# Four graph layers, two batches in flight: the last layer's second values, queries and keys through the other accumulators, and a new order

## The chip, the cores and the metric

The kernel runs on one core of a Trainium2 chip. The number is the device time of one launch in microseconds (us), the median of several runs. The core has a matrix engine (TensorE, PE in the rows; its weight loads are PEld), VectorE (DVE), ScalarE (ACT), GpSimd (POOL), and SyncE (SP), which issues transfers. Each engine works through its own instructions strictly in order and meets the others only at semaphores.

## The reference, cut to what matters

16 batches of 512 nodes with 256 features pass through four layers, each followed by a residual sum and a layer norm.

```python
x = _layernorm(x + _L0_gnn_ref(x, adj, w, a1, a2))      # attention from two scores per node, elu
x = _layernorm(x + _L1_gnn_ref(x, adj, ...))             # 3 times: attention, norm, 256-1024-256 gelu ffn, norm
x = _layernorm(x + _L2_gnn_ref(x, adj, W, a))            # like L0, keeping the 16 largest weights of a row
x = _layernorm(x + _L3_gnn_ref(x, adj, Wq, Wk, Wv, Wo))  # 8 heads of 32 features
...
q = heads(x @ Wq); k = heads(x @ Wk); v = heads(x @ Wv)
scores = jnp.einsum('bhnd,bhmd->bhnm', q, k) / sqrt_dk
attn = jax.nn.softmax(jnp.where(mask, scores, -jnp.inf), axis=-1)
out = jnp.einsum('bhnm,bhmd->bhnd', attn, v)
return jax.nn.relu(out) @ Wo
```

## The kernel before

**Tiles.** A batch is four row tiles of 128 nodes; tiles 0 and 1 are half 0, tiles 2 and 3 half 1. All of a batch's work is cut into named *stages*, such as `v1` (the values of half 1) or `pT0` (transposing the weights of tile 0). Each engine has a table from stage names to the code that it runs for them; a stage in which an engine has no part is skipped there.

**Two batches in flight.** Two slots, A and B, each hold one batch with buffers of its own (in printed rows, the first number of `work_1_0` or `acc_1_0` is the slot, and the one in `XT_1` too; the profile leaves these numbers out). The list `HALF` is one half turn: the batch in one slot does its *middle* (layer L0, then L1.0, then L1.1 and the first attention of L1.2), while the batch in the other slot does its *ending* (the ffn of L1.2, L2, L3) and the next one is *starting*. The order of the entries of `HALF` is the order of the instructions on every engine, so moving one entry moves it on all that take part. A turn runs `to_a`, then `to_b`, seven times in a loop, with an opening half turn (middle alone, mostly) ahead, and a closing one behind, which is followed by an ending that runs alone. That makes 16 half turns with a middle in them, of which 15 also have an ending.

**Banks.** TensorE writes to eight banks: for each slot, two *work* banks, used in strict alternation in the order of the list `uses` (class `Use`), and two *accumulators* (`acc`), used in the order of `acc_uses`. Before TensorE writes to a bank it waits until the engine that read the last contents has freed it (`evacuated`), and readers wait for `filled`. In L3 the head scores of a *quad* (four heads by one row tile) need all four banks of the slot at once: `sq{q}` on TensorE writes them, `sq{q}` and `sr{q}` on VectorE add the mask and take the row minimum (line 867), `ex{n}` on ScalarE is the exponential (line 1036), `uT{n}` transposes a head's weights (line 1270), and `pv{g}` multiplies them by the values (line 1289).

**Around the change.** `qk0` and `qk1` compute the queries and keys of feature chunk 0 and 1 (four heads each, line 1238). ScalarE copies the queries out (line 1025), VectorE the keys (`keys`, line 854). `v0` and `v1` compute the values (line 1130, copied by ScalarE, line 956). Before, all of them go through the two work banks, and in that list `v1`, `q`, `k` of chunk 1 stand behind `scores 0`, the first quad. The middle's stages next to them are those of L1.1: `sx1` (node scores on VectorE, line 671), `bc` (their broadcast by TensorE, line 1161), `zs0`/`zs1` (sums on ScalarE, line 964), `mx0`/`mx1` (mask, row minimum, leaky relu on VectorE, lines 692 to 704), `exp0`/`exp1` (line 978), `pT0` to `pT3` (transposes, line 1173, copied by lines 752 and 986), `agg0`/`agg1` (weights times rows, line 1187). The ffn's stages are `hT` (transpose, line 1103), `f1hq` (first product, half h, quarter q, line 1209, gelu on line 1018), and `f2hq` (second product, line 1223). `sum`, `norm`, `xsum`, `xnorm` are sums with statistics, and normalizations, on VectorE, with a power on GpSimd between them (line 510); `xa1` is an affine step on GpSimd (lines 518, 522), in L1.0 with an addition to all of `X1` behind it (line 560). `masks` and `load` belong to the transfers.

## Time and profile before

| what | value |
| --- | --- |
| time, median of 3 runs | 3801.18 us (3792.32 to 3809.88) |
| the profiled execution | 3815.43 us, of which 3813.8 us from the first to the last instruction |
| mean granted TensorE clock | 0.961 of full speed |
| TensorE busy | 3324.7 us, 87% |
| VectorE busy | 2460.1 us, 65% |
| ScalarE busy | 2204.2 us, 58% |
| GpSimd busy | 773.0 us, 20% |
| table loads on ScalarE | 198 |

TensorE is busy for most of the span, so its idle times, and the stretches at the lower clock, are what an order can change. The others' shares are averages over stages in which sometimes one and sometimes another of them is what TensorE waits for. A "half turn" in the rows is the stretch from one `v1` of L0 to the next.

### The profile page before, as it was taken

What the parts mean: (1) busy time and instruction counts of PE and PEld (TensorE: products, weight loads), DVE (VectorE), ACT (ScalarE), POOL (GpSimd) and SP (SyncE); (2) the same over time, 40 slices, a digit from 0 to 9 for tenths busy, and PEclk for the clock granted to TensorE, in tenths of its full rate; (3) what the DMA queues carried; (4) which work ended last, traced back from release to release, by engine and by line L of the source; (5) the groups of instructions that cost most, each with busy time, mean ns of one, the idle gap of its engine ahead of it and who ended that gap; (6) DMA issues with size and microseconds to landing.
All of it is one profiled execution on the core that took longest, in us unless ns stands there. A gap on an engine that the chain in (4) does not pass through costs nothing.

```text
span 3813.8 us, 59841 instructions
## 1 busy us (share of the span) xinstructions
PE 3324.7 (87%) x18048; PEld 2558.3 (67%) x18048; DVE 2460.1 (65%) x7151; ACT 2204.2 (58%) x4349; POOL 773.0 (20%) x1052
## 2 busy tenths in 40 slices
PE   6689989898898899889998898989989898899866
PEld 4576766767667676666766677676766766667653
DVE  3466676666757666676666767666676666767654
ACT  3256556665565756656665575756656665565623
POOL 1212122121211222121121212122121121211210
PEclk8899999999999999999999999999999999999988
DMA  5000000000000000000000000000000000000000
GB/s 137 1 1 12 7 12 7 7 7 7 12 7 10 3 7 12 7 12 7 7 7 7 12 7 12 1 7 12 7 12 7 7 6 7 12 7 1 1 6 6
DMA packets 39858, 40.24 MB, mean 11 GB/s; under 512 B 7264, under 2 KB 38240, under 8 KB 39520
## 3 DMA queue, kind: packets, MB, share of 16 engines
q1 hardware_dynamic: 31072, 27.68, 2.4%
q0 software_dynamic: 8448, 8.39, 1.5%
q8 instruction: 170, 2.79, 0.3%
q14 instruction: 168, 1.38, 0.1%
HBM read 36.07 MB, written 8.39 MB: 12 GB/s over the span
## 4 chain that ended last, share of the span: by engine, by line
PE 48%; issue 25%; ACT 11%; DVE 11%; POOL 4%; DVEq 0%; DMA 0%; POOLq 0%; ACTq 0%; SPq 0%
PE acc L1187 11%; PE work L1209 9%; PE acc L1223 7%; PE acc L1289 3%; PE work L1130 3%; ACT PT L1036 3%; PE acc L1258 3%; POOL rstd L510 2%; PE acc L1270 2%; PE acc L1318 2%; PE work L1103 2%; PE work L1238 2%; ACT L1036 2%; PE work L1173 1%; DVE stats L759 1%
## 5 line engine op out<-in xcount | busy, mean ns | idle before, releaser
L1209 PE MATMUL work<-XT,w_sb 128*128 128x256 f32 x3072 | 732.7, 384 | 36.7 <-DVE XT L816 15.0
L510 POOL TENSOR_TENSOR rstd<-var_eps,minus_half 128x2 f32<-128x2 f32 x320 | 225.1, 703 | 2641.4 <-DVE var_eps L768 2641.2
L1223 PE MATMUL acc<-w_sb,gT 128*128 128x256 f32 x3072 | 731.4, 385 | 0.0
L1209 PEld LDWEIGHTS work<-XT,w_sb 128*128 128x128 f32 x3072 | 557.6, 190 | 168.2 <-ACT gT L1018 35.5
L1223 PEld LDWEIGHTS acc<-w_sb,gT 128*128 128x128 f32 x3072 | 579.9, 193 | 97.8 <-issue 22.8
L1018 ACT ACTIVATE gT<-work,b_sb 128x256 f32<-128x256 f32 x768 | 343.1, 473 | 208.6 <-PE work L1209 201.1
L1187 PE MATMUL acc<-X,PT 128*128 128x256 f32 x1536 | 387.6, 410 | 24.8 <-ACT PT L986 24.2
L1187 PEld LDWEIGHTS acc<-X,PT 128*128 128x128 f32 x1536 | 312.7, 207 | 108.8 <-issue 46.3
L1018 ACT ACT_TABLE_LOAD x198 | 254.0, 1283 | 3.5
L752 DVE COPY PT<-work 128x512 f32<-128x512 f32 x160 | 109.5, 684 | 225.5 <-PE work L1173 223.8
L759 DVE BATCH_NORM_STATS2 stats<-R 128x6 f32<-128x256 f32 x640 | 240.9, 418 | 11.0
L1173 PE MATMUL work<-ident,T 128*128 128x128 f32 x1280 | 184.1, 282 | 72.9 <-ACT T L978 56.6
L1187 PE MATMUL acc<-V,PT 128*128 128x256 f32 x1024 | 235.8, 383 | 3.9 <-ACT PT L986 3.7
L1173 PEld LDWEIGHTS work<-ident,T 128*128 128x128 f32 x1280 | 146.8, 143 | 123.2 <-ACT T L978 91.2
L699 DVE SCALAR_TENSOR_TENSOR T<-T 128x512 f32<-128x512 f32 x320 | 225.3, 708 | 0.0
L1258 PE MATMUL acc<-X,R 32*128 32x512 f32 x512 | 154.7, 678 | 75.9 <-DVE X L854 44.4
L692 DVE CUSTOM_DVE_ANT_0 T<-T,pos 128x512 f32<-128x512 f32 x256 | 186.9, 766 | 50.5 <-ACT T L964 50.2
L1187 PEld LDWEIGHTS acc<-V,PT 128*128 128x128 f32 x1024 | 196.1, 192 | 33.3 <-issue 4.5
L978 ACT ACTIVATE T<-T,neg_max 128x512 f32<-128x512 f32 x256 | 182.4, 713 | 59.4 <-DVE neg_max L704 59.0
L1047 ACT ACTIVATE PT<-acc 128x512 f32<-128x512 f32 x128 | 76.1, 594 | 241.7 <-PE acc L1270 241.7
L956 ACT ACTIVATE V<-work 128x258 f32<-128x258 f32 (+1 forms) x192 | 74.1, 386 | 234.5 <-PE work L1130 234.5
L986 ACT ACTIVATE PT<-work 128x512 f32<-128x512 f32 x160 | 93.9, 587 | 172.1 <-PE work L1173 170.9
(153 smaller groups left out, 5934.7 us busy)
## 6 DMA issues: line engine op xcount, KB each, us to landing
HX<-in_x SPq DMA_DIRECT2D x16, 512.0 KB, 3.8
pos<-in_adj POOLq DMA_DIRECT2D x16, 512.0 KB, 5.7
out<-X SPq DMA_DIRECT2D x32, 256.0 KB, 2.1
w_sb<-in_L_gnn_W SPq DMA_DIRECT2D x6, 1024.0 KB, 8.4
g_sb<-in_L_gnn_g SPq DMA_DIRECT2D x6, 128.0 KB, 6.7
awr_sb<-in_L_gnn_attn_w SPq DMA_DIRECT2D x2, 256.0 KB, 7.9
c_sb<-in_L_gnn_beta SPq DMA_DIRECT2D x3, 128.0 KB, 4.5
PT<-in_L_gnn_b SPq DMA_DIRECT2D x3, 128.0 KB, 5.7
```

The source lines that it names most:

```text
L510: pool.tensor_tensor(rstd[s][:, half_rows(half)], var_eps[s][:, half_rows(half)], minus_half[:], ALU.pow)\
L692: dve.tensor_tensor_reduce(T[s][:, t, :], T[s][:, t, :], pos[s][:, t, :], 1.0, HIGHEST, ALU.add, ALU.min, neg_row[s][:, t:t + 1]).then_inc ...
L699: dve.scalar_tensor_tensor(T[s][:, t, :], T[s][:, t, :], ALPHA[key], T[s][:, t, :], ALU.mult, ALU.max if key == "L2" else ALU.min).then_in ...
L759: last = dve.bn_stats(stats[s][:, t, :], R[s][:, t, :])
L978: act.activation(to, T[s][:, t, :], ACT.Exp, bias=neg_max[s][:, t:t + 1], scale=1.0 if key == "L2" else -1.0, accum_out=den[s][:, t:t + 1] ...
L1018: act.activation(gT[s][:, f, :], u.bank[:, 0:HN], ACT.Gelu, bias=b1_sb[:, l, f:f + 1]).then_inc(u.evacuated, 1)
L1036: act.activation(z, z, ACT.Exp, bias=head_min[s][:, n:n + 1], scale=-1.0, accum_out=den3[s][:, m, half * HT + i, r:r + 1]).then_inc(exp_do ...
L1173: last = pe.transpose(u.bank[:, j * P:(j + 1) * P], T[s][:, t, j * P:(j + 1) * P], ident[:])
L1187: last = pe.matmul(acc[s][half][:, t % HT, :], PT[s][:, j, t * P:(t + 1) * P], src[s][:, j, 0:D], start=(j == 0 and t % HT == 0), stop=(j ...
L1209: last = pe.matmul(u.bank[:, 0:HN], w1_sb[:, l, c, f * P:(f + 1) * P], XT[s][:, c, half * HN:(half + 1) * HN], start=(c == 0), stop=(c == ...
L1223: last = pe.matmul(acc[s][half][:, i, :], gT[s][:, f, i * P:(i + 1) * P], w2_sb[:, l, f, :], start=(f == 0 and i == 0), stop=(f == FC - 1) ...
L1258: pe.matmul(use.bank, q_sb[s][rows, m, t * P:(t + 1) * P], k_sb[s][rows, m, :], start=True, stop=True).then_inc(use.filled, 1)
```

## The change

Three things.

1. `v1` of L3 no longer uses the work banks: its two tiles go to the slot's two accumulators. So do the queries and the keys of chunk 1. In `uses`, these four entries are gone, and the two `q`/`k` entries that stay are those of chunk 0; in `acc_uses`, `v1 L3` and `qk1 L3` stand ahead of `scores 0`.
2. Since the banks are used in list order, `v1` and `qk1` now come ahead of the first quad `sq0` in `HALF`.
3. The rest of `HALF` is in a new order too, in about twenty places. The stages and the work in them are the same.

```diff
-        ("middle", "L1.0", "xnorm1"), ("ending", "L3", "qk0"), ("middle", "L1.1", "sx1"),
-        ("ending", "L3", "sq0 sr0"), ("middle", "L1.0", "xa1"), ("middle", "L1.1", "bc zs0 mx0"),
-        ("ending", "L3", "v1"), ("middle", "L1.1", "zs1 exp0 mx1"), ("ending", "L3", "qk1"),
...
+        ("middle", "L1.1", "sx1"), ("ending", "L3", "load qk0 v1 qk1 sq0 sr0"), ("middle", "L1.0", "xa1"),
+        ("middle", "L1.1", "bc zs0 mx0 zs1 exp0"), ("ending", "L3", "ex0"), ("middle", "L1.1", "mx1"),
...
-        uses += [("xT0 L3", DC), ("v0 L3", HT), ("xT1 L3", DC), ("q L3", 1), ("k L3", 1), ("scores 0", 2), ("v1 L3", HT), ("q L3", 1), ("k L3", 1)]
+        uses += [("xT0 L3", DC), ("v0 L3", HT), ("xT1 L3", DC), ("q0 L3", 1), ("k0 L3", 1), ("scores 0", 2)]
...
-        acc_uses = [(k, 1) for k in ["L0"] + [k + c for k in L1K for c in ("", " ffn")] + ["L2"]] + [("scores 0", 1)]
+        acc_uses = [(k, 1) for k in ["L0"] + [k + c for k in L1K for c in ("", " ffn")] + ["L2"]]
+
+        acc_uses += [("v1 L3", 1), ("qk1 L3", 1), ("scores 0", 1)]
...
+        def query_or_key(s, it, m, i):
+
+            return HeadUse(s, it, 2 + i, ("q0 L3", "k0 L3")[i], 0) if m == 0 else HeadUse(s, it, i, "qk1 L3")
...
             def keys(m):
                 def stage(s, it, key):
-                    u = Use(s, it, "k L3", m)
-                    dve.wait_ge(u.filled, u.turn)
-                    dve.tensor_copy(k_sb[s][:, m, :], u.bank[:]).then_inc(u.evacuated, 1)
+                    use = query_or_key(s, it, m, 1)
+                    dve.wait_ge(use.filled, use.filled_at)
+                    dve.tensor_copy(k_sb[s][:, m, :], use.bank).then_inc(use.evacuated, 1)
...
                     for t in tiles(half):
-                        u = Use(s, it, "v L0", t) if key == "L0" else Use(s, it, f"v{half} {key}", t % HT)
-                        pe.wait_ge(u.evacuated, u.turn)
+                        if key == "L3" and half == 1:
+                            use = HeadUse(s, it, t % HT, "v1 L3")
+                            pe.wait_ge(use.evacuated, use.free)
+                            bank, made = use.bank, use.filled
```

**First place, TensorE, the start of L3 in slot 1.** Before, behind the first queries and keys come the first quad (line 1258, to all four banks), the broadcast of L1.1 in slot 0 (line 1161), and only then the values (line 1130), which need a work bank of the quad back.

```order
L1238 MATMUL work_1_0<-XT_1,wq_sb 128x512 x2
L1238 MATMUL work_1_1<-XT_1,wk_sb 128x512 x2
...
L1258 MATMUL work_1_0<-X_1,R_1 128x512
L1258 MATMUL work_1_1<-X_1,R_1 128x512
L1152 REGISTER_ALU
L1161 MATMUL work_0_1<-ident,s12_0 128x128 x4
L1128 REGISTER_ALU
L1130 MATMUL work_1_0<-wv_sb,XT_1 128x256 x2
L1130 MATMUL work_1_1<-wv_sb,XT_1 128x256 x2
L1236 REGISTER_ALU
L1238 MATMUL work_1_0<-XT_1,wq_sb 128x512 x2
L1238 MATMUL work_1_1<-XT_1,wk_sb 128x512 x2
```

The same engine and place with the change (the same lines have other numbers in the changed file: values 1145, queries and keys 1253, quad 1273, broadcast 1176, transposes of L1.1 1188).

```order
L1253 MATMUL work_1_1<-XT_1,wk_sb 128x512 x2
...
L1145 MATMUL acc_1_0<-wv_sb,XT_1 128x256 x2
...
L1253 MATMUL acc_1_0<-XT_1,wq_sb 128x512 x2
L1251 REGISTER_ALU
L1253 MATMUL acc_1_1<-XT_1,wk_sb 128x512 x2
...
L1273 MATMUL work_1_1<-X_1,R_1 128x512
L1167 REGISTER_ALU
L1176 MATMUL work_0_1<-ident,s12_0 128x128 x4
L1184 REGISTER_ALU
L1188 MATMUL work_0_0<-ident,T_0 128x128 x4
```

The values and the second queries and keys, which stood between the broadcast and the transposes of L1.1, stand ahead of the quad now, and nothing is left between the broadcast and the transposes that wait for its results.

**Second place, ScalarE, L0 of slot 0 beside the ffn of L1.2 in slot 1.** Before, the sums of tiles 0 and 1 (line 964, `zs0`) stand ahead of the gelus of `f102` (line 1018), and those of tiles 2 and 3 (`zs1`) behind them.

```order
L1008 ACTIVATE XT_1<-work_1_1,beta1t_sb,g1t_sb 128x256
L962 REGISTER_ALU
L964 ACTIVATE T_0<-work_0_0,V_0 128x512 x2
L1017 REGISTER_ALU
L1018 ACTIVATE gT_1<-work_1_1,b1_sb 128x256
L1017 REGISTER_ALU
L1018 ACTIVATE gT_1<-work_1_0,b1_sb 128x256
L964 ACTIVATE T_0<-work_0_0,V_0 128x512 x2
L968 ISA
L1018 ACTIVATE gT_1<-work_1_1,b1_sb 128x256
```

With the change (sums 973, gelu 1027):

```order
L1017 ACTIVATE XT_1<-work_1_1,beta1t_sb,g1t_sb 128x256
L971 REGISTER_ALU
L973 ACTIVATE T_0<-work_0_0,V_0 128x512 x4
L977 ISA
L1026 REGISTER_ALU
L1027 ACTIVATE gT_1<-work_1_1,b1_sb 128x256
L1026 REGISTER_ALU
L1027 ACTIVATE gT_1<-work_1_0,b1_sb 128x256
L1027 ACTIVATE gT_1<-work_1_1,b1_sb 128x256
```

All four sums now run ahead of the first gelu of `f102`. On TensorE, their broadcast `bc` of L0 has moved from behind `hT1` to between `hT0` and `f100`.

**Third place, TensorE, L1.0 of slot 0 beside L2 of slot 1.** Before, the values of L2 (line 1130) stand ahead of `agg1` of L1.0 (line 1187).

```order
L1103 MATMUL work_1_0<-ident,X1_1 128x128 x2
L1119 REGISTER_ALU
L1130 MATMUL work_1_1<-wg_sb,XT_1 128x258 x2
L1130 MATMUL work_1_0<-wg_sb,XT_1 128x258 x2
L1179 REGISTER_ALU
L1187 MATMUL acc_0_1<-X1_0,PT_0 128x256 x4
L1185 REGISTER_ALU
L1187 MATMUL acc_0_1<-X1_0,PT_0 128x256 x4
```

With the change (transposes 1112, values 1145, `agg1` 1202):

```order
L1112 MATMUL work_1_0<-ident,X1_1 128x128 x2
L1194 REGISTER_ALU
L1202 MATMUL acc_0_1<-X1_0,PT_0 128x256 x4
L1200 REGISTER_ALU
L1202 MATMUL acc_0_1<-X1_0,PT_0 128x256 x4
L1209 REGISTER_ALU
L1112 MATMUL work_0_1<-ident,HX_0 128x128 x2
L1112 MATMUL work_0_0<-ident,HX_0 128x128 x2
L1128 REGISTER_ALU
L1145 MATMUL work_1_1<-wg_sb,XT_1 128x258 x2
L1145 MATMUL work_1_0<-wg_sb,XT_1 128x258 x2
```

The values moved behind `agg1` and `hT0` of L1.0. On VectorE, at the same time, `sum0` of L1.0 goes ahead of L2's copy of `XT`, and `mx0` of L2 goes behind `norm1` and `hT1` of L1.0. A little later `f203` goes ahead of `agg0` of L2.

## Rows read from the trace of the kernel before

**Rows 1.** The page's first part: busy time, share, instructions of TensorE.
```profile
PE 3324.7 (87%) x18048; PEld 2558.3 (67%) x18048; DVE 2460.1 (65%) x7151; ACT 2204.2 (58%) x4349; POOL 773.0 (20%) x1052
```
**Rows 2.** Windows of two half turns: stretch, its length, busy times, granted clock.
```profile
887.70:1118.20 230.50, 206.70 (x1130) 158.85 (x1128) 154.15 (x448) 139.69 (x274) 48.86 (x66) 0.97 0.03 8
1806.40:2034.20 227.80, 203.60 (x1129) 157.47 (x1128) 154.16 (x449) 139.69 (x274) 49.11 (x67) 0.99 0.03 8
```
**Rows 3.** Timeline of TensorE, start of L3: start, length, what [idle before, releaser].
```profile
1000.39 1.95 PE L1238 MATMUL work<-XT,wq_sb 128*128 128x512 f32 x4 [0.56 <-DVE XT L654]
...
1005.23 0.70 PE L1258 MATMUL acc<-X,R 32*128 32x512 f32 x2 [1.17 <-DVE X L854]
...
1006.42 0.65 PE L1161 MATMUL work<-ident,s 128*128 128x128 f32 x4
1008.49 1.99 PE L1130 MATMUL work<-wv_sb,XT 128*128 128x256 f32 x8 [1.42 <-DVE head_min L867]
1010.32 1.88 PE L1238 MATMUL work<-XT,wq_sb 128*128 128x512 f32 x4
...
1013.83 0.66 PE L1173 MATMUL work<-ident,T 128*128 128x128 f32 x4
1015.03 0.66 PE L1173 MATMUL work<-ident,T 128*128 128x128 f32 x4 [0.55 <-ACT T L978]
1017.38 1.22 PE L1258 MATMUL acc<-X,R 32*128 32x512 f32 x2 [1.70 <-DVE X L854]
...
1019.40 5.88 PE L1187 MATMUL acc<-X,PT 128*128 128x256 f32 x16
```
**Rows 4.** Timeline of VectorE at the same place.
```profile
1006.51 0.69 DVE L867 CUSTOM_DVE_ANT_0 T<-acc,pos 128x512 f32<-128x512 f32 x1
...
1008.96 1.04 DVE L692 CUSTOM_DVE_ANT_0 T<-T,pos 128x512 f32<-128x512 f32 x1
...
1013.99 0.68 DVE L692 CUSTOM_DVE_ANT_0 T<-T,pos 128x512 f32<-128x512 f32 x1
...
1016.56 0.68 DVE L854 COPY X<-work 128x512 f32<-128x512 f32 x1
```
**Rows 5.** Timeline of ScalarE at the same place.
```profile
1014.16 0.72 ACT L978 ACTIVATE T<-T,neg_max 128x512 f32<-128x512 f32 x1 [0.39 <-DVE neg_max L704]
...
1016.06 0.72 ACT L978 ACTIVATE T<-T,neg_max 128x512 f32<-128x512 f32 x1 [0.60 <-DVE neg_max L704]
...
1017.48 0.57 ACT L986 ACTIVATE PT<-work 128x512 f32<-128x512 f32 x1
```
**Rows 6.** A window at the same place: length, busy times, granted clock.
```profile
1017.00:1023.80 6.80, 6.42 (x18) 4.08 (x19) 3.48 (x11) 3.88 (x11) 0.00 (x0) 0.50 0.00 1
```
**Rows 7.** Timeline of TensorE, L0 beside the ffn of L1.2.
```profile
890.91 3.72 PE L1209 MATMUL work<-XT,w_sb 128*128 128x256 f32 x16 [0.64 <-DVE XT L816]
...
895.91 3.88 PE L1209 MATMUL work<-XT,w_sb 128*128 128x256 f32 x16
...
902.61 1.43 PE L1173 MATMUL work<-ident,T 128*128 128x128 f32 x8 [1.10 <-ACT T L978]
```
**Rows 8.** Timeline of ScalarE at the same place.
```profile
895.11 0.56 ACT L1008 ACTIVATE XT<-work,beta1t_sb,g1t_sb 128x256 f32<-128x256 f32 x1
896.11 1.27 ACT L964 ACTIVATE T<-work,V 128x512 f32<-128x512 f32 x2 [0.43 <-PE work L1161]
...
900.45 1.28 ACT L978 ACT_TABLE_LOAD   x1
```
**Rows 9.** Timeline of TensorE, L1.0 beside L2.
```profile
959.15 1.99 PE L1209 MATMUL work<-XT,w_sb 128*128 128x256 f32 x8 [0.95 <-ACT gT L1018]
962.00 0.66 PE L1103 MATMUL work<-ident,HX 128*128 128x128 f32 x4 [0.86 <-DVE HX L773]
```
**Rows 10.** Timeline of ScalarE, L2's first aggregation read out.
```profile
984.77 0.60 ACT L986 ACTIVATE PT<-work 128x512 f32<-128x512 f32 x1
```
**Rows 11.** Timeline of TensorE, the ending that runs alone.
```profile
3733.11 2.91 PE L1130 MATMUL work<-wv_sb,XT 128*128 128x256 f32 x8 [2.21 <-DVE head_min L867]
```

More of the change, by code:

```diff
@@ L349, in build, with __init__ @@
         class HeadUse:
-            def __init__(self, s, it, place, name):
+            def __init__(self, s, it, place, name, n=None):
                 if place < 2:
@@ L358, in __init__ @@
                 else:
[L359 removed]
+                    u = Use(s, it, name, place - 2 if n is None else n)
                     self.bank, self.filled, self.filled_at = u.bank[:], u.filled, u.turn
                     self.evacuated, self.free, self.done = u.evacuated, u.turn, u.turn + 1
+        def query_or_key(s, it, m, i):
+            return HeadUse(s, it, 2 + i, ("q0 L3", "k0 L3")[i], 0) if m == 0 else HeadUse(s, it, i, "qk1 L3")
         def target_score(s, key, t):
@@ L952, in stage @@
                     for t in tiles(half):
+                        if key == "L3" and half == 1:
+                            use = HeadUse(s, it, t % HT, "v1 L3")
+                            act.wait_ge(use.filled, use.filled_at)
+                            act.activation(V[s][:, t, 0:D], use.bank[:, 0:D], ACT.Copy).then_inc(use.evacuated, 1)
+                            continue
                         u = Use(s, it, "v L0", t) if key == "L0" else Use(s, it, f"v{half} {key}", t % HT)
@@ L1022, in stage @@
                 def stage(s, it, key):
-                    u = Use(s, it, "q L3", m)
-                    act.wait_ge(u.filled, u.turn)
-                    act.activation(q_sb[s][:, m, :], u.bank[:], ACT.Copy, scale=-float(DK) ** -0.5).then_inc(u.evacuated, 1)
+                    use = query_or_key(s, it, m, 0)
+                    act.wait_ge(use.filled, use.filled_at)
+                    act.activation(q_sb[s][:, m, :], use.bank, ACT.Copy, scale=-float(DK) ** -0.5).then_inc(use.evacuated, 1)
                 return stage
@@ L1126, in stage @@
                     for t in tiles(half):
-                        u = Use(s, it, "v L0", t) if key == "L0" else Use(s, it, f"v{half} {key}", t % HT)
-                        pe.wait_ge(u.evacuated, u.turn)
+                        if key == "L3" and half == 1:
+                            use = HeadUse(s, it, t % HT, "v1 L3")
+                            pe.wait_ge(use.evacuated, use.free)
+                            bank, made = use.bank, use.filled
+                        else:
+                            u = Use(s, it, "v L0", t) if key == "L0" else Use(s, it, f"v{half} {key}", t % HT)
+                            pe.wait_ge(u.evacuated, u.turn)
+                            bank, made = u.bank, u.filled
                         for c in range(DC):
-                            last = pe.matmul(u.bank[:, 0:columns], XT[s][:, c, t * P:(t + 1) * P], weights[:, c, 0:columns],
+                            last = pe.matmul(bank[:, 0:columns], XT[s][:, c, t * P:(t + 1) * P], weights[:, c, 0:columns],
                                              start=(c == 0), stop=(c == DC - 1))
-                        last.then_inc(u.filled, 1)
+                        last.then_inc(made, 1)
                 return stage
@@ L1233, in stage @@
                         wait_transposed(s, it, key, 1)
-                    for name, w in (("q", wq_sb), ("k", wk_sb)):
-                        u = Use(s, it, f"{name} L3", m)
-                        pe.wait_ge(u.evacuated, u.turn)
+                    for i, w in enumerate((wq_sb, wk_sb)):
+                        use = query_or_key(s, it, m, i)
+                        pe.wait_ge(use.evacuated, use.free)
                         for c in range(DC):
-                            last = pe.matmul(u.bank[:], w[:, c, m * P:(m + 1) * P], XT[s][:, c, :],
+                            last = pe.matmul(use.bank, w[:, c, m * P:(m + 1) * P], XT[s][:, c, :],
                                              start=(c == 0), stop=(c == DC - 1))
-                        last.then_inc(u.filled, 1)
+                        last.then_inc(use.filled, 1)
                 return stage
@@ L1247, in stage @@
                     if q % (NQ // DC) == 0:
-                        for name in "qk":
-                            use = Use(s, it, f"{name} L3", m)
-                            pe.wait_ge(use.evacuated, use.turn + 1)
+                        for part in range(2):
+                            use = query_or_key(s, it, m, part)
+                            pe.wait_ge(use.evacuated, use.done)
                     places = [HeadUse(s, it, r, f"scores {q}") for r in range(HPC)]
```

1 line of the change is left out of this document (removed), and 101 rows, old and new, of the table HALF.

## The prediction

> **What bounds the kernel now.** First read the page: TensorE is busy for 3324.7 of 3813.8 us [rows 1], so it is the engine whose idle time and clock the order can change. Next cut the span into half turns. Two of them, 230.50 and 227.80 us long [rows 2], do the same work; TensorE is busy for 206.70 us in one and 203.60 in the other, at a granted clock of 0.97 and 0.99. So some 24 us of a half turn are idle, and a further 3 come and go with the clock. Then read TensorE's timeline at the places that the change touches, asking for each idle stretch what ends it, and read VectorE and ScalarE beside it: what counts is which of them is late.
>
> At the start of L3 [rows 3] the idle stretches are 1.17 us (the key copy, line 854), 1.42 (the row minima of the quad, line 867, that hold the work banks), 0.55 (an exponential of L1.1), and 1.70 (the second key copy). VectorE is what is late: from the first row minimum at 1006.51 [rows 4] to the key copy at 1016.56 it has one operation behind another. Behind the four idle stretches the granted clock is 0.50, its lower level of 1.2 GHz, for the whole window from 1017.0 to 1023.8 [rows 6], and `agg0` of L1.1 takes 5.88 us [rows 3], where its 16 products last some 3.6 at full clock, by the x16 row of 3.72 of the same shape [rows 7].
>
> **The change, part by part.** All times are of the half turn that the rows show, and "shift" is how much later a stage comes with the change.
>
> *The start of L3.* The same products are issued, in as many instructions; nothing is removed but two waits. The 1.42 us wait for the row minima goes, since the values use banks long free, and the 1.70 us wait goes, since the second keys are copied before the quad. But two things are lost. The copy of the second keys must now be over before the quad starts, which is the 1.17 us wait again, only later. And the values with the second queries and keys took from 1008.49 to 1013.83, 5.3 us [rows 3], between the broadcast and `pT0`, in which sums, mask and exponential of L1.1 ran. With the change nothing is left there. Step by step, with the shift at entry set to nought: first queries and keys from 1000.4, 3.5 us (as 1010.32 to 1013.83), to 1003.9; values 1.8 (1008.49 to 1010.32), to 1005.7; second queries and keys 3.5, to 1009.2; wait 1.2; quad 1.2 (1005.23 to 1006.42), to 1011.6; broadcast 0.6, to 1012.2. VectorE's first row minimum comes 1.3 us after the quad's start (1005.23 in [rows 3], 1006.51 in [rows 4]), so at 1011.7, and the four take 2.45 (1006.51 to 1008.96), to 1014.15. Then `mx0`, in the same order on VectorE as before: an undisturbed `mx` takes 2.57 us (1013.99 to 1016.56 in [rows 4]), and the first exponential starts 2.07 us after its beginning (1013.99 there, 1016.06 in [rows 5]). So exponential at 1016.2, and `pT0` 0.87 later (1014.16 in [rows 5], 1015.03 in [rows 3]), at 1017.1. TensorE is idle from 1012.2 to 1017.1, 4.9 us. `mx1` ends at 1014.15 + 5.15 = 1019.3; ScalarE's copy of `pT0` starts 0.92 after the end of `mx1` (1016.56 in [rows 4], 1017.48 in [rows 5]), lasts 0.57, and `agg0` starts at 1020.9. Before, it started at 1019.40 [rows 3]. So this place costs 1.5 us by itself.
>
> In this sum `mx0` runs undisturbed. Before, its first operation took 1.04 us, where the same in `mx1` takes 0.68 [rows 4]; GpSimd's additions to `X1` (line 560) ran then. They follow `sx1`, which now comes before the key copies, so they are over by about 1012. If they were not, the price would be that of `mx0` before, 5.03 us (1008.96 to 1013.99) less 2.57, so 2.5 more. The Trainium skill (SBUF — State Buffer, "SBUF: two separate sides") says that VectorE with two inputs in SBUF and GpSimd hold a shared port pair in turn, and that the other fully blocks. The trace shows a stretched operation beside GpSimd, as that rule has it, but by less than a full GpSimd operation; by the rule alone the sum would be the 2.5 higher if the two met again.
>
> *L1.0 beside L2.* The values of L2 stood in front of `agg1` of L1.0; now they stand behind `hT0`, and fill the time in which its transpose is waited for. `mx0` of L2 leaves its place ahead of `norm1` of L1.0, which `hT1` waited 0.86 us for, after 0.95 ahead of `f101` [rows 9]. `agg1` comes earlier by the values' 1.8 us and by the 0.5 us that they waited for their copy; of `f101`'s and `hT1`'s waits about 1.4 us go, and new ones of 0.5 (ahead of `hT0`) and of 0.6 (a gelu now behind the sums) come. With the values themselves paid later, `f102` comes about 2.5 us earlier. Not all stays. `f203` now stands ahead of `agg0` of L2, so `agg0` ends only 0.7 us or so earlier, and ScalarE's read of it, a table load of 1.28, and the copy of `pT2` (984.77, 0.60 long) [rows 10] follow it; `agg1` of L2 needs that copy. I get 1.0 us of new idle time there. So L3 begins with a shift of -1.5.
>
> *L0 beside the ffn of L1.2.* The broadcast now fills 0.43 us of the 0.64 us gap ahead of `f100` [rows 7]. But on ScalarE all four sums come before the first gelu of `f102`. They start when the copy of `hT1` is done, 895.67 [rows 8], and two take 1.27, four 2.4, so to 898.1. The gelu then frees its bank at 898.6; `f103`, which is the second half of the x16 row at 895.91 and began at 897.8 [rows 7], needs it. It comes 0.8 us later, its last gelu ends at 901.05, and the table load for the exponential starts then, not at 900.45 [rows 8]: +0.6 for `pT0` of L0, which already waited for it (1.10 us in [rows 7]). TensorE is busy from there on, so +0.6 stays.
>
> *The small swaps* (`uT8`, `uT18`, `pT2`, `ex14` and the like), one price together: ScalarE and VectorE have slack where these stand, so they are taken at nothing, except `uT8`, whose earlier place pushes `hT1` of L1.1 against a gelu: +0.2. Without that slack each would cost one copy, about 0.6 us [rows 10].
>
> *The ending that runs alone.* There the wait ahead of the values is 2.21 us [rows 11], with no middle to hide it; the same walk gives about -1 once.
>
> **The sum.** Per half turn +0.6 (L0) -1.5 (to the start of L3) +1.5 (start of L3) +0.2 = +0.8. Fifteen half turns have both parts: +12, and -1 for the last ending, so +11 us: 3824.8 for the profiled span of 3813.8. The profiled execution lies 14 us above the median of the runs shown, 3801.18, so the forecast is 3801.18 + 11 = **3812 us**. In this the clock's loss is left as it is. That is the largest unknown: the lower clock now costs about 5.88 - 3.6 = 2.3 us at `agg0` and 0.9 at the slowed quad ahead of it. With more of TensorE's idle time in one piece it may fall earlier, inside that piece, and cost less, or last longer. Bounds: all of the 2.3 gained, or, as much again lost.
>
> **The rivals.**
>
> *The lower clock falls into the new idle stretch (faster).* For it: the stretch of 4.9 us comes before the place where the clock fell, so `agg0` could run at full clock again. Against it: there is still idle time right ahead of `agg0`. Price: -2.3 in each of 15 half turns, -35: 3777 us. It decides for faster once more than 2.0 us per half turn come back in this way.
>
> *The lower clock lasts longer (slower).* Here the 4.9 us bring the clock down earlier and the second idle piece, between the second quad and `agg0`, keeps it down: `agg0` in full and the first transposes at half speed, +1.5 per half turn; and the few half turns that now keep their clock, like that of 227.80 us [rows 2], lose their 2.7 us too (three or so, 8 us). 15 x 1.5 + 8 = 30 on top of 11: 3842 us. The Trainium skill (TensorE: Matmul & The Clock Gate, "What's actually happening") says the gate follows how busy the array has been recently. By that rule a longer idle piece speaks for this rival; that the clock fell behind four idle stretches here agrees [rows 3, 6].
>
> *Nothing much at all (no change).* The 1.5 us lost at the start of L3 rest on VectorE starting the minima only after the late quad. If the walk misses 0.8 us per half turn, from L0's gelu and from there, the time is 3801. This is also the case that the change does what it says, removing the two waits, and the removed time turns up as one wait for `pT0`.
>
> **How the numbers follow.** I give the forecast (3800 to 3824 for its own range, half a microsecond or so per half turn either way) 0.37, no change at all 0.17, the clock falling earlier 0.22, the clock lasting longer 0.24. A measurement of this kernel tells about 0.5%, 19 us, from no change: under 3782 counts as faster, over 3820 as slower. Faster takes the first rival and a little of the rest, 0.24; slower takes the second and the upper end of the forecast, 0.33; the remaining 0.43 is same. The range for 8 in 10 runs from the first rival's price, 3775, to the second's, 3842.
>
> **What would show it.** Right: no wait of the values for line 867's successor any more; an idle stretch of 4 to 6 us ahead of `pT0` of L1.1, ended by ScalarE's exponential; the second quad without a wait; `f103` of L1.2 waiting about 1 us for a gelu; `hT1` of L1.0 about 2 us earlier in the half turn. Half turns of about 231 us. Wrong: the idle ahead of `pT0` stays under 3 us, which would mean VectorE reaches `mx0` sooner than the walk has it; or the granted clock at `agg0` of L1.1 is at its full level in most half turns.

## The result, and the profile after

The changed kernel takes **3819.67 us** (median of 12 runs, 3812.31 to 3827.39), the kernel before 3801.69 us beside it (12 runs, 3790.56 to 3809.88): a ratio of **1.0051**, 95% interval 1.0038 to 1.0065, so 18 us slower where 11 were forecast.

The profiled execution of before (3815.43 us) lies above all 12 timed runs of before, so its span and that of the changed kernel's profile (3818.62 us, near its median) are only 3 us apart. Its waits are those of other executions, but its mean clock (0.961) is under that of all 10 runs of `same_again`. Another execution of the kernel before, `same_again` (3796.67 us, span 3795.0), is the fairer partner for totals, and is used so below.

First the page of the changed kernel, which answers to [rows 1]:

```profile
span 3817.0 us, 59925 instructions
PE 3338.0 (87%) x18048; PEld 2564.3 (67%) x18048; DVE 2417.6 (63%) x7151; ACT 2198.5 (58%) x4349; POOL 747.7 (20%) x1052
```

And that of the kernel before in its other execution:

```profile
span 3795.0 us, 59841 instructions
PE 3311.0 (87%) x18048; PEld 2555.5 (67%) x18048; DVE 2459.8 (65%) x7151; ACT 2204.3 (58%) x4349; POOL 773.7 (20%) x1052
```

Subtract TensorE's busy time from the span: it idles for 479.0 us after the change and 484.0 before it. Idle time went down by 5 us. The same 18048 instructions were busy for 27 us longer. The granted clock went down with it (mean 0.952 to 0.957 in the 12 runs of the changed kernel, 0.962 to 0.966 in the 10 of `same_again`), by about 1%, and 27 us are 0.8% of the busy time. So the loss is one of clock.

TensorE's timeline of the changed kernel at the start of L3, to be laid beside [rows 3] (columns: start, length, what, idle before it and its releaser):

```profile
994.39 1.95 PE L1253 MATMUL work<-XT,wq_sb 128*128 128x512 f32 x4 [0.56 <-DVE XT L658]
...
997.90 1.89 PE L1145 MATMUL acc<-wv_sb,XT 128*128 128x256 f32 x8
999.63 1.88 PE L1253 MATMUL acc<-XT,wq_sb 128*128 128x512 f32 x4
1001.35 1.88 PE L1253 MATMUL acc<-XT,wk_sb 128*128 128x512 f32 x4
1004.01 0.70 PE L1273 MATMUL acc<-X,R 32*128 32x512 f32 x2 [0.79 <-DVE X L858]
...
1005.08 0.65 PE L1176 MATMUL work<-ident,s 128*128 128x128 f32 x4
1010.72 1.97 PE L1188 MATMUL work<-ident,T 128*128 128x128 f32 x8 [4.98 <-ACT T L987]
1012.62 1.22 PE L1273 MATMUL acc<-X,R 32*128 32x512 f32 x2
...
1014.72 4.70 PE L1202 MATMUL acc<-X,PT 128*128 128x256 f32 x16
```

The waits of 1.42, 0.55 and 1.70 us are gone, that of 1.17 is 0.79, and 4.98 us stand ahead of `pT0`. From the first queries to `agg0` it takes 20.33 us; before, 19.01 [rows 3].

VectorE there, beside [rows 4]: the minima start when the late quad is there, and `mx0` (line 696) runs undisturbed.

```profile
1003.26 0.69 DVE L858 COPY X<-acc 128x512 f32<-128x512 f32 x1 [2.85 <-PE acc L1253]
1005.32 0.69 DVE L871 CUSTOM_DVE_ANT_0 T<-acc,pos 128x512 f32<-128x512 f32 x1 [1.36 <-PE acc L1273]
1007.77 0.69 DVE L696 CUSTOM_DVE_ANT_0 T<-T,pos 128x512 f32<-128x512 f32 x1
```

The clock of the changed kernel in windows (start and end, length, busy time of PE, PEld, DVE, ACT, POOL, then the granted clock, the DMA share and GB/s), to be laid beside [rows 2] and [rows 6]:

```profile
1003.20:1009.90 6.70, 1.75 (x13) 0.72 (x12) 5.27 (x16) 2.48 (x5) 2.40 (x4) 1.00 0.00 0
1009.90:1016.70 6.80, 5.96 (x21) 3.70 (x22) 5.58 (x17) 6.18 (x17) 0.00 (x0) 0.50 0.00 1
1016.70:1023.50 6.80, 6.36 (x45) 5.08 (x43) 3.25 (x10) 3.60 (x10) 0.00 (x0) 1.00 0.00 0
881.70:1112.10 230.40, 206.86 (x1131) 159.35 (x1129) 151.38 (x449) 139.35 (x275) 47.19 (x66) 0.97 0.03 8
```

The clock is at its upper level for most of the idle stretch (which runs from 1005.73 to 1010.72) and falls to 1.2 GHz 0.8 us before its end. It stays there over `pT0`, `pT1`, the second quad and the first products of `agg0`, and is back for the rest of `agg0`. The same holds in all 14 half turns that follow the first: the clock falls inside the idle stretch, 0.1 to 2.9 us before its end.

L0 on TensorE and ScalarE, beside [rows 7, 8]:

```profile
893.06 1.99 PE L1224 MATMUL work<-XT,w_sb 128*128 128x256 f32 x8 [0.98 <-ACT gT L1027]
897.75 1.43 PE L1188 MATMUL work<-ident,T 128*128 128x128 f32 x8 [0.96 <-ACT T L987]
```

```profile
889.93 2.41 ACT L973 ACTIVATE T<-work,V 128x512 f32<-128x512 f32 x4
892.53 0.84 ACT L1027 ACTIVATE gT<-work,b_sb 128x256 f32<-128x256 f32 x2 [0.18 <-ACT T L973]
895.58 1.28 ACT L987 ACT_TABLE_LOAD   x1
```

The four sums run for 2.41 us, `f103` waits 0.98 us for the gelu behind them, and `pT0` of L0 starts 16.05 us after the half turn's start at 881.70, where it was 14.91 (902.61 in [rows 7] less 887.70 in [rows 2]): +1.14.

### The profile page after: what moved, and what is told of

It reads as the page before. It is cut to its first block, busy times and chain, and to the rows that moved or that the text cites. A ratio compares the mean times of both kernels' runs of the same rounds, so it can differ in the third digit from the quotient of the medians.

```text
span 3817.0 us, 59925 instructions
## 1 busy us (share of the span) xinstructions
PE 3338.0 (87%) x18048; PEld 2564.3 (67%) x18048; DVE 2417.6 (63%) x7151; ACT 2198.5 (58%) x4349; POOL 747.7 (20%) x1052
## 4 chain that ended last, share of the span: by engine, by line
PE 42%; issue 33%; DVE 10%; ACT 9%; POOL 5%; DVEq 0%; DMA 0%; POOLq 0%; ACTq 0%; SPq 0%
PE acc L1238 8%; PE work L1224 5%; PE acc L1202 5%; PE acc L1304 3%; PE acc L1273 3%; POOL rstd L514 3%; PE work L1145 3%; ACT PT L1045 2%; PE acc L1333 2%; PE acc L1285 2%; PE work L1188 2%; PE work L1112 2%; PE work L1253 2%; DVE stats L763 2%; ACT L1045 2%
## 5 line engine op out<-in xcount | busy, mean ns | idle before, releaser
L1202 PE MATMUL acc<-X,PT 128*128 128x256 f32 x1536 | 371.1, 397 | 25.0 <-ACT PT L995 24.8
L1202 PEld LDWEIGHTS acc<-X,PT 128*128 128x128 f32 x1536 | 298.8, 199 | 105.3 <-ACT PT L995 32.9
L1188 PE MATMUL work<-ident,T 128*128 128x128 f32 x1280 | 204.9, 296 | 143.5 <-ACT T L987 124.2
L1188 PEld LDWEIGHTS work<-ident,T 128*128 128x128 f32 x1280 | 159.9, 151 | 189.4 <-ACT T L987 144.9
L703 DVE SCALAR_TENSOR_TENSOR T<-T 128x512 f32<-128x512 f32 x320 | 217.3, 683 | 0.0
L973 ACT ACTIVATE T<-work,s 128x512 f32<-128x512 f32 x192 | 116.2, 690 | 121.8 <-PE work L1176 121.8
```

What stands on the lines that cost most here:

```text
L703: dve.scalar_tensor_tensor(T[s][:, t, :], T[s][:, t, :], ALPHA[key], T[s][:, t, :], ALU.mult, ALU.max if key == "L2" else ALU.min).then_in ...
L1188: last = pe.transpose(u.bank[:, j * P:(j + 1) * P], T[s][:, t, j * P:(j + 1) * P], ident[:])
L1202: last = pe.matmul(acc[s][half][:, t % HT, :], PT[s][:, j, t * P:(t + 1) * P], src[s][:, j, 0:D], start=(j == 0 and t % HT == 0), stop=(j ...
```

## The experiments

The theory (the "order theory" of the expectations) was the prediction's: three sites of +0.6, -1.5 and +1.5 us per half turn, limited at the start of L3 by VectorE's queue. The rivals: the clock alone (the "clock theory"); no effect of an order; the broadcast, which comes too late behind the quad, as the limit. Ratios are to the kernel before on the same chip (3793.36 us in the first set, 3800.25 in the second, 3796.69 in the third).

### First set: the parts apart

`same_again` is the kernel before, unchanged.

> The kernel before, unchanged, to see how far its own executions lie apart in the granted clock. Both theories: ratio 1.000 within 0.002. The order theory says that the places of the lower clock are the same in every execution (agg0 of L1.1 in most half turns), the clock theory that some executions lose it in fewer half turns, with a time some 10 us under the 3815 us of the profiled execution shown.

Measured 1.0012 (0.9994 to 1.0030): no difference.

`l0_back` is the changed kernel with the old order of L0:

```diff
-        ("middle", "L0", "v1"), ("ending", "L1.2", "hT0 ha0"), ("middle", "L0", "bc"),
-        ("ending", "L1.2", "sum1 norm1 f100 f101 hT1 ha1"), ("middle", "L0", "zs0 mx0 zs1"),
-        ("ending", "L1.2", "f102 f103"), ("middle", "L0", "exp0"), ("ending", "L1.2", "f200"),
+        ("middle", "L0", "v1"), ("ending", "L1.2", "hT0 ha0 sum1 norm1 f100 f101 hT1"),
+        ("middle", "L0", "bc zs0"), ("ending", "L1.2", "ha1"), ("middle", "L0", "mx0"),
+        ("ending", "L1.2", "f102"), ("middle", "L0", "zs1"), ("ending", "L1.2", "f103"),
...
```

> The changed kernel with the old order in L0 alone (the stages ahead of L2's xT0). Order theory: the comparison of the two traces puts TensorE 1.1 us later at the end of this part in every half turn, so undoing it gives back 15 to 16 times 1.1, 17 us: about 3803 us, ratio 1.000. Clock theory (the loss is the clock's alone, from the 5 us idle stretch in L3): no more than 4 us come back, 3816 us, ratio 1.004.

Measured 1.0028 (1.0013 to 1.0043), against 1.0051 for the whole change: the order of L0 costs about 0.0023, 9 us, which is the forecast's 15 times 0.6. The two intervals just overlap, so this size is a rough one. The order theory's 1.000 lies outside the interval, since the rest of the change costs more than it had. The clock theory's 1.004 lies inside it, but that theory has no place for a loss in L0 itself, which the waits show (the 0.98 us of `f103` are gone from TensorE's rows of `l0_back`).

`acc_alone` is the change with the old order everywhere except at the start of L3:

```diff
-        ("middle", "L1.0", "xnorm1"), ("ending", "L3", "qk0"), ("middle", "L1.1", "sx1"),
-        ("ending", "L3", "sq0 sr0"), ("middle", "L1.0", "xa1"), ("middle", "L1.1", "bc zs0 mx0"),
-        ("ending", "L3", "v1"), ("middle", "L1.1", "zs1 exp0 mx1"), ("ending", "L3", "qk1"),
+        ("middle", "L1.0", "xsum1 xnorm1"), ("middle", "L1.1", "sx1"),
+        ("ending", "L3", "load qk0 v1 qk1 sq0 sr0"), ("middle", "L1.0", "xa1"),
+        ("middle", "L1.1", "bc zs0 mx0 zs1 exp0"), ("ending", "L3", "ex0"), ("middle", "L1.1", "mx1"),
```

> The kernel before with the accumulators for v1 and qk1 and the changed order from xsum1 of L1.0 to the second quad of L3, and the old order everywhere else. Order theory: agg0 of L1.1 starts 1.6 us later per half turn, 15 times that is +24 us, less 1.0 to 1.5 us per half turn for an agg0 at the full clock: 3803 to 3811 us, ratio 1.000 to 1.0025. If TensorE's clock brings no relief: 3825 us, 1.006. If VectorE's removed waits counted for themselves (1.4 + 1.7 us less idle time per half turn): 3755 us, 0.988.

Measured 1.0100 (1.0067 to 1.0133): 38 us, over all three expectations. TensorE's timeline shows the same walk as in the whole change, with `agg0` at full clock here:

```profile
1017.43 1.97 PE L1190 MATMUL work<-ident,T 128*128 128x128 f32 x8 [4.98 <-ACT T L989]
1019.33 1.22 PE L1275 MATMUL acc<-X,R 32*128 32x512 f32 x2
...
1021.44 3.72 PE L1204 MATMUL acc<-X,PT 128*128 128x256 f32 x16
```

Again 20.33 us from the queries (at 1001.11) to `agg0`. Against `same_again`, TensorE idles 15.5 us more (499.5 of 3835.1) and is busy 24.6 us more (3335.6). The idle part is the walk's, somewhat less than the 22 us forecast; the busy part is the clock. What the walk stands against is seen in TensorE's rows of `same_again`:

```profile
995.78 1.96 PE L1238 MATMUL work<-XT,wq_sb 128*128 128x512 f32 x4 [0.56 <-DVE XT L654]
...
1012.77 0.70 PE L1258 MATMUL acc<-X,R 32*128 32x512 f32 x2 [1.70 <-DVE X L854]
...
1013.84 3.72 PE L1187 MATMUL acc<-X,PT 128*128 128x256 f32 x16
```

There it is 18.06 us, with the second quad 0.70 and `agg0` 3.72, not 1.22 and 5.88 as in [rows 3]. The waits of the stretch add up to 5.77 us after the change (0.79 and 4.98) and 4.83 in `same_again` (1.17, 1.41, 0.55 and 1.70). So of the 2.27 us between 18.06 and 20.33 some 0.9 are idle time and the rest, about 1.3, is that of the halved clock on the transposes and the second quad. Read over the 14 half turns that follow the first, `agg0` of L1.1 lasts over 5 us in 11 of them in the profile of before, in 6 in `same_again`, and in none in the changed kernel; the stretch to it is 20.3 us long in 13 of the changed kernel's and 18.1 or 18.2 in 9 of those of `same_again`. And `proj0` with `pv3`, late in the half turn, last 6.2 us on average in the changed kernel, 5.5 in `same_again`.

`l1_order_alone` is the kernel before with the new order from `xT0` of L2 to `xT1` of L3 alone:

```diff
-        ("middle", "L1.0", "agg0 pT2 pT3"), ("ending", "L2", "xT1 v1"),
-        ("middle", "L1.0", "sum0 norm0 agg1 hT0 ha0 sum1"), ("ending", "L2", "bc zs0 mx0"),
-        ("middle", "L1.0", "norm1 f100 f101 hT1"), ("ending", "L2", "zs1"),
+        ("middle", "L1.0", "pT2 pT3 sum0"), ("ending", "L2", "xT1"),
+        ("middle", "L1.0", "norm0 agg1 hT0 ha0"), ("ending", "L2", "v1"),
+        ("middle", "L1.0", "sum1 norm1 f100"), ("ending", "L2", "bc zs0"),
+        ("middle", "L1.0", "f101 hT1 ha1"), ("ending", "L2", "mx0 zs1"),
...
```

> The kernel before with the changed order of L1.0 and L2 alone (xT0 of L2 to xT1 of L3). Order theory: 2.0 us per half turn gained there, as the two traces stand, and kept: 3801.7 - 31 = 3771 us, ratio 0.992. Rival: L3's start is bound by VectorE, which takes the gain back as idle time of TensorE ahead of the quad: 3800 us, ratio 1.000.

Measured **0.9931** (0.9908 to 0.9954): 26 us faster, as the order theory had it, and its rival's 1.000 falls. This part of the change is good by itself. The three parts also add up: -0.0069, +0.0100 and +0.0023 make +0.0054, and the whole change measured +0.0051.

### Second set: what limits the start of L3

All four stand on `l0_back` (1.0028). `bc_only` puts the broadcast and its first sums ahead of the second queries and keys; `bc_mask_early` puts `mx0` ahead of them too; `agg_first` and `agg_first_b` bring the transposes and `agg0` of L1.1 ahead of the quad's follow-up. The lines are those of `l0_back` in `HALF`; below them stand the stages of the same stretch in each run, in short form.

```diff
-        ("ending", "L3", "load qk0 v1 qk1 sq0 sr0"), ("middle", "L1.0", "xa1"),
-        ("middle", "L1.1", "bc zs0 mx0 zs1 exp0"), ("ending", "L3", "ex0"), ("middle", "L1.1", "mx1"),
...
```

```text
bc_only:       load qk0 v1 | xa1 | bc zs0 | qk1 sq0 sr0 | mx0 zs1 exp0 | ex0 | mx1 | ex1 | exp1 pT0 pT1
bc_mask_early: load qk0 v1 | xa1 | bc zs0 mx0 | qk1 sq0 sr0 | zs1 exp0 | ex0 | mx1 | ex1 | exp1 pT0 pT1
agg_first:     load qk0 v1 | xa1 | bc zs0 mx0 | qk1 | zs1 exp0 pT0 mx1 pT1 | sq0 sr0 | exp1 agg0 | ex0 ex1
agg_first_b:   load qk0 v1 | xa1 | bc zs0 mx0 | qk1 | zs1 exp0 pT0 pT1 | sq0 sr0 ex0 | mx1 | ex1 | exp1 agg0
```

> The kernel with L0's old order, and in L3's start the broadcast of L1.1 and the sums of zs0 moved ahead of the second queries and keys; VectorE's order is as in the change. If VectorE's late start (second key copy, then quad, minima, mask) sets when agg0 begins, the empty stretch on TensorE only moves, and the ratio stays at 1.003, as without this move. If what costs is that nothing hides the chain broadcast, sums, mask, exponential, this start of it 4 us earlier brings 3 us or so per half turn: ratio 0.991.

Measured 1.0044 (1.0025 to 1.0063). The broadcast came 5 us earlier and `pT0` no sooner, 17.0 us behind the first queries (at 997.61) where it was 16.3:

```profile
1003.06 0.65 PE L1180 MATMUL work<-ident,s 128*128 128x128 f32 x4
...
1007.93 0.70 PE L1277 MATMUL acc<-X,R 32*128 32x512 f32 x2 [0.79 <-DVE X L862]
...
1014.64 1.97 PE L1192 MATMUL work<-ident,T 128*128 128x128 f32 x8 [5.56 <-ACT T L991]
```

It is VectorE, which takes the quad's minima (from 1009.24) and only then `mx0` (from 1011.69), that `pT0` waits for. The theory of the broadcast fell.

> As bc_only, and the mask and leaky relu of tiles 0 and 1 (mx0) ahead of the second key copy on VectorE, where the change leaves VectorE idle for some 2.9 us. If VectorE's total work between sx1 and agg0 is the limit: mx0 fills the idle time, but runs beside GpSimd's additions and is stretched, the key copy and quad come later, net 0 to 1 us per half turn: ratio 0.999 to 1.003. If the empty stretch ahead of pT0 itself is the cost, 4 to 5 us per half turn go: 0.985.

Measured 1.0068 (1.0046 to 1.0090): a miss, above both expectations. TensorE's rows (first queries at 999.86):

```profile
1012.29 0.70 PE L1277 MATMUL acc<-X,R 32*128 32x512 f32 x2 [2.89 <-DVE X L862]
...
1013.36 1.64 PE L1192 MATMUL work<-ident,T 128*128 128x128 f32 x8
...
1020.17 5.59 PE L1206 MATMUL acc<-X,PT 128*128 128x256 f32 x16 [1.81 <-ACT PT L999]
```

`pT0` comes 2.8 us earlier than in `l0_back` and the first quad 2.8 us later, and `agg0` starts 20.3 us behind the queries, as it did without the move. That is what a limit in VectorE's total work predicts. But `agg0` now lasts 5.4 us or more in all 14 half turns, where it was 3.7 to 4.5 in `l0_back`. TensorE idles 8.5 us more (480.8 against 472.3) and is busy 18.4 more (3346.9 against 3328.5): the larger part of this loss is the clock's.

> The quad's minima are taken out of agg0's way: sq0 and its minima come behind the masks and transposes of L1.1 (VectorE: mx0, key copy, mx1, copy of pT1, then minima), and the second quad behind agg0, so that the product of 3.6 us runs while VectorE works through the minima. Order theory (VectorE's queue ahead of agg0 is the cost): agg0 starts some 5 us earlier, part of it given back before agg1, 3 to 5 us per half turn: ratio 0.983 to 0.991. Rival: the heads' chain becomes late instead and takes it all back: 1.003.

Measured 1.0059 (1.0035 to 1.0083); the rival's side, and above it. TensorE's idle time fell to 458.0 us from the 472.3 of `l0_back`, and `agg0` starts 14.4 us behind the queries in most half turns and not 20.3, so the order did what it was meant to do. But TensorE's busy time rose from 3328.5 to 3372.5, at a mean clock of 0.947 in the profiled execution against 0.955: the loss is mostly one of clock. VectorE's and GpSimd's rows show why the idle time fell by no more:

```profile
1009.58 1.21 DVE L699 CUSTOM_DVE_ANT_0 T<-T,pos 128x512 f32<-128x512 f32 x1
...
1011.84 0.67 DVE L711 SCALAR_TENSOR_TENSOR neg_max<-neg_row 128x1 f32<-128x1 f32 x1
```

```profile
1011.34 4.18 POOL L567 TENSOR_TENSOR X<-X,beta_sb 128x256 f32<-128x256 f32 x4
```

`mx0` has met GpSimd's affine step (1009.03 to 1011.37) and its additions to `X1` again; 0.69 became 1.21. And behind it the heads' chain is late:

```profile
1027.96 1.33 PE L1288 MATMUL work<-ident,T 128*128 128x128 f32 x8 [1.36 <-DVE head_min L874]
1030.16 1.16 PE L1276 MATMUL acc<-X,R 32*128 32x512 f32 x2 [0.88 <-DVE PT L885]
...
1033.05 1.97 PE L1288 MATMUL acc<-ident,PT 128*128 128x128 f32 x8 [0.84 <-DVE head_min L874]
```

> As agg_first, but the minima of the first quad ahead of mx1, so that agg0 waits for both on VectorE and the heads' exponentials start earlier. Order theory: agg0 comes 2.4 us later than in agg_first, while the heads are earlier: 1 to 3 us per half turn better than L0's old order alone, ratio 0.990 to 0.998. Rival as there: 1.003.

Measured 1.0146 (1.0118 to 1.0174), the worst of all; a miss. `agg0` starts as early as in `agg_first` (14.4 us behind the queries), but in the half turn read above the second quad comes 2.4 us later (21.4 against 19.0), with an idle stretch of 1.91 us ahead of `pT2`. Against `l0_back` TensorE idles only 3.8 us more (476.0) and is busy 56.5 more (3385.0): nearly all of this loss too is in the busy time, at a mean clock of 0.946. So in the last three of these four runs the larger part of the loss against `l0_back` is in TensorE's busy time, and not in its waits.

### Third set: the values alone, and GpSimd's additions out of the way

`v1_alone` has only `v1` in the accumulators, in the order of before but with `v1` behind `qk0`:

```diff
-        ("middle", "L1.0", "xnorm1"), ("ending", "L3", "qk0"), ("middle", "L1.1", "sx1"),
-        ("ending", "L3", "sq0 sr0"), ("middle", "L1.0", "xa1"), ("middle", "L1.1", "bc zs0 mx0"),
-        ("ending", "L3", "v1"), ("middle", "L1.1", "zs1 exp0 mx1"), ("ending", "L3", "qk1"),
...
+        ("ending", "L3", "qk0 v1"), ("middle", "L1.1", "sx1"), ("ending", "L3", "sq0 sr0"),
+        ("middle", "L1.0", "xa1"), ("middle", "L1.1", "bc zs0 mx0 zs1 exp0 mx1"), ("ending", "L3", "qk1"),
...
-        uses += [("xT0 L3", DC), ("v0 L3", HT), ("xT1 L3", DC), ("q L3", 1), ("k L3", 1), ("scores 0", 2), ("v1 L3", HT), ("q L3", 1), ("k L3", 1)]
+        uses += [("xT0 L3", DC), ("v0 L3", HT), ("xT1 L3", DC), ("q0 L3", 1), ("k0 L3", 1), ("scores 0", 2), ("q1 L3", 1), ("k1 L3", 1)]
...
+        acc_uses += [("v1 L3", 1), ("scores 0", 1)]
```

> The kernel before with only v1 of L3 through the accumulators and ahead of the first quad; the second queries and keys stay in the work banks and behind the quad, and the order is the old one elsewhere. If VectorE's queue from the first quad's minima to agg0 is what bounds this stretch: the values (1.8 us) fill TensorE's 1.17 us gap ahead of the quad, but the quad starts 0.6 us later and so does all behind it, up to +9 us, ratio 1.000 to 1.0025. If TensorE's idle time counts for itself: 1.2 us less per half turn, 3783 us, ratio 0.995.

Measured 1.0051 (1.0028 to 1.0074): the sign of the VectorE theory, twice its size.

```profile
1001.90 1.98 PE L1256 MATMUL work<-XT,wq_sb 128*128 128x512 f32 x4 [1.56 <-DVE head_min L874]
...
1006.89 1.36 PE L1191 MATMUL work<-ident,T 128*128 128x128 f32 x8 [1.28 <-ACT T L990]
1009.91 1.22 PE L1276 MATMUL acc<-X,R 32*128 32x512 f32 x2 [1.66 <-DVE X L861]
...
1011.93 5.83 PE L1205 MATMUL acc<-X,PT 128*128 128x256 f32 x16
```

The wait for the minima is merely handed to the queries (1.56 us), and TensorE's idle time is that of `same_again` within a microsecond (484.9 and 484.0). Its busy time is 17.7 us more (3328.7), and `agg0` lasts 4.9 us or more in 13 of 14 half turns; the mean clock of its 7 runs is 0.958 to 0.963, under most of those of `same_again`. So between these two executions the loss is the clock's, and not the later start that the VectorE theory had: its sign was right for another reason.

`shift_late` is `l1_order_alone` with GpSimd's four additions to `X1` moved from behind `xa1` to behind `mx1`, where VectorE has done with its masks:

```diff
-                    if key == L1K[0] and half == 1:
-                        for t in range(NT):
-                            last = pool.tensor_tensor(X1[s][:, t, :], X1[s][:, t, :], beta2_sb[:, L - 1, :], ALU.add)
-                        last.then_inc(x1_shifted.sems[s], 1)
...
+            def shift_x1(s, it, key):
+                if key == L1K[1]:
+                    pool.wait_ge(lrelu_done.sems[s], lrelu_done.value(it, key, NT - 1))
+                    for t in range(NT):
+                        last = pool.tensor_tensor(X1[s][:, t, :], X1[s][:, t, :], beta2_sb[:, L - 1, :], ALU.add)
+                    last.then_inc(x1_shifted.sems[s], 1)
...
+            stages = {"load": load_next, "mx1": shift_x1, ...
```

> The kernel before with the changed order of L1.0 and L2 (as l1_order_alone, 0.993), and GpSimd's four additions to X1 after VectorE's masks of L1.1 and not beside them. If the stretched mask operations (5.0 us for mx0, where mx1 takes 2.6) are on the path: agg0 of L1.1 starts 1.5 to 2.5 us earlier, ratio 0.983 to 0.987. If TensorE would not be free for it, or the additions only stretch what comes behind: 0.993.

Measured **0.9818** (0.9791 to 0.9844), 3727.8 us: 69 us faster than the kernel before, and by the ratios 2.3% under the changed kernel, a little better than expected. Against `l1_order_alone` TensorE idles 23.7 us less (429.5 of 3723.0 against 453.2 of 3763.0) and is busy 16.3 less (3293.5 against 3309.8). What it removed stands in VectorE's and GpSimd's rows of `l1_order_alone`:

```profile
994.83 1.20 DVE L695 CUSTOM_DVE_ANT_0 T<-T,pos 128x512 f32<-128x512 f32 x1
...
997.09 0.68 DVE L707 SCALAR_TENSOR_TENSOR neg_max<-neg_row 128x1 f32<-128x1 f32 x1
```

```profile
994.30 4.65 POOL L563 TENSOR_TENSOR X<-X,beta_sb 128x256 f32<-128x256 f32 x4
```

and what it left, in those of `shift_late`:

```profile
986.22 0.68 DVE L698 CUSTOM_DVE_ANT_0 T<-T,pos 128x512 f32<-128x512 f32 x1
...
987.44 0.14 DVE L710 SCALAR_TENSOR_TENSOR neg_max<-neg_row 128x1 f32<-128x1 f32 x1
```

```profile
990.84 2.78 POOL L567 TENSOR_TENSOR X<-X,beta_sb 128x256 f32<-128x256 f32 x4 [5.10 <-DVE T L705]
```

VectorE is 34 us less busy in all (2415.1 against 2449.2), and TensorE's timeline of `shift_late` shows what that frees:

```profile
976.69 1.95 PE L1244 MATMUL work<-XT,wq_sb 128*128 128x512 f32 x4 [0.56 <-DVE XT L660]
...
984.79 1.99 PE L1136 MATMUL work<-wv_sb,XT 128*128 128x256 f32 x8 [1.42 <-DVE head_min L873]
...
990.05 1.04 PE L1179 MATMUL work<-ident,T 128*128 128x128 f32 x8
991.58 0.70 PE L1264 MATMUL acc<-X,R 32*128 32x512 f32 x2 [0.49 <-DVE X L860]
```

The wait of 1.42 us that the change set out to remove is still there; the 0.55 is gone and the 1.70 is 0.49. `agg0` starts 16.0 us after the queries and lasts 3.7 us in all 14 half turns; the lower clock does not appear in this stretch in any of them.

`shift_late_bc0` adds the early broadcast of L0 (behind `ha0` of L1.2), without the new order of the gelus:

> As shift_late, and the broadcast of L0 between hT0 and f100 as in the change, with ScalarE's sums and gelus in the old order. It splits the change's two edits in L0: if the gelu behind all four sums was the cost, the broadcast alone fills a part of the 0.64 us gap and gains 0.2 to 0.4 us per half turn, ratio 0.001 to 0.002 under shift_late's. If the early broadcast itself was what cost, it is some 0.004 above.

Measured 0.9818 (0.9792 to 0.9844), 3729.58 us: no difference. The 0.004 that the broadcast would have cost is not there, so what L0 lost in the change points to the gelu behind four sums. No run has that order alone, and a gain of 0.001 to 0.002 could not be told from none.

`shift_late_key` puts `qk1` of L3 right behind `v1`, so that the key copy comes ahead of `mx1`:

> As shift_late, with VectorE's second key copy ahead of mx1 and not behind it, so that the second quad (which waited 1.70 us for it) can follow pT1 at once. VectorE has the same work ahead of the copy of pT1, so agg0 cannot come earlier than that allows: 0 to 1 us per half turn better than shift_late, 0 to 0.004 under its ratio. If the wait of the second quad counted in full, 1.7 us per half turn, 0.007 under.

Measured 0.9904 (0.9879 to 0.9929), 0.009 over `shift_late`: a miss. VectorE now stands idle in front of the copy:

```profile
998.47 0.69 DVE L859 COPY X<-work 128x512 f32<-128x512 f32 x1 [1.99 <-PE work L1243]
999.08 0.68 DVE L697 CUSTOM_DVE_ANT_0 T<-T,pos 128x512 f32<-128x512 f32 x1
```

It waits 1.99 us for a product, with `mx1` queued behind, and TensorE then waits 1.18 us ahead of `pT0` and 1.15 ahead of `agg0`.

## Why the prediction came out as it did

The table sets its terms (us in the whole run, 15 half turns) beside TensorE's idle and busy time, each from one profiled execution: L1.0/L2 is `l1_order_alone` less `same_again`, the start of L3 is `acc_alone` less `same_again`, L0 is the changed kernel less `l0_back` (472.3 idle, 3328.5 busy), and the rest is the remainder. Two executions of the kernel before differ by 5.1 in idle and 13.7 in busy time ([rows 1] and `same_again`), so only large entries of the last column count.

The sum of the idle and the busy column, 22 us, is the difference of these two spans (3817.0 and 3795.0); the medians are 18 us apart.

| term | forecast | idle | busy |
| --- | --- | --- | --- |
| L0 | +9 | +6.7 | +9.5 |
| L1.0 beside L2 | -22 | -30.8 | -1.2 |
| start of L3 | +22 | +15.5 | +24.6 |
| small swaps, last ending | +2 | +3.6 | -5.9 |
| sum | +11 | -5.0 | +27.0 |

- **L0 (+0.6 per half turn).** Right in mechanism: `f103` waits 0.98 us for its gelu. The shift is 1.1 us at `pT0`; 9 us by the ratios.
- **L1.0 beside L2 (-1.5).** Right, a little more: `hT1` of L1.0 starts 73.4 us into the half turn (955.08 less 881.70), before 74.3 (962.00 in [rows 9] less 887.70 in [rows 2]), although L0 sent it 1.1 later, so 2.0 us are gained; by itself the part is worth 26 us, 1.7 a half turn.
- **Start of L3 (+1.5).** The walk was right: 20.5 us forecast from the queries to `agg0` (1000.4 to 1020.9), 20.33 measured, with 4.98 us ahead of `pT0` for the 4.9 forecast. That `mx0` would be undisturbed was right too (0.69 us, not 1.04).
- **The small swaps and the last ending (+2).** Not tested by themselves; the remainder in the table is smaller than what two executions of one kernel differ by.
- **The clock's loss, "left as it is".** This is the term that was mis-sized: nought forecast, about +25 us measured. Two errors sit in it. The walk was set against rows in which the second quad already ran at the lower level (19.01 us); in `same_again` that is so in 5 of 14 half turns, and the price against its 18.06 is 2.3, not 1.3. And the low clock did not stay where it was: it moved from `agg0` onto `pT0`, `pT1` and the second quad, there in every half turn where before it struck in some, and lasts longer at `proj0` and `pv3`. What `agg0` gave back, 0.7 us on average against `same_again`, is about what `proj0` and `pv3` took (also 0.7).
- **The rivals.** The clock falling earlier, into the idle stretch, did happen, in all 14 half turns, and `agg0` ran at or near full clock (3.7 to 3.8 us) in 9 of them. But the fall came only 0.1 to 2.9 us before the stretch's end, so the lower clock lay on `pT0`, `pT1` and the second quad, and the gain of 35 us that the rival had did not come. The clock lasting longer half happened: its first transposes at half speed are there and its price of 30 us was near the 25 measured, but `agg0` recovered, against its wording. The sign that the prediction set down as showing it wrong, `agg0` at full clock in most half turns, did appear, and with it the size of its clock term fell. The total was still near, by luck: the idle terms came out 16 us lower than forecast and the clock 27 higher, and the two errors cancel for the most part. That nothing much would change did not come true either: L0 and the start of L3 lost as the walk had it.

By the Trainium skill (TensorE: Matmul & The Clock Gate, "What's actually happening") the gate follows how busy the array has been recently. The windows agree as far as they go: the lower clock sets in late in the 5 us of idle time. What stays open is why, in the order of before, the same waits bring the low clock in some half turns and not in others, and whether the longer low stretch at `proj0` follows from the start of L3; no run here separates these. Nor does a run show whether spreading the same idle time would bring the clock back: in `shift_late`, where it is back, idle time was removed as well.

## What to carry to other kernels

A wait that a new order removes can come back elsewhere when the engine that was late still has the same work to do: at the start of L3 VectorE was late, and neither free banks nor an earlier broadcast helped, while taking GpSimd off VectorE's back made the kernel 1.1% faster than the same order without it. An order can still be worth having where it fills a wait with other work, as in L1.0. Split a difference into TensorE's idle and busy time before explaining it, and read the clock of several executions of the unchanged kernel before pricing a walk against one of them. And when one change bundles several orders, run the parts: a gain of 0.7% was hidden in one that lost 0.5%.
